# The gate's third tanh written in place in PSUM: a small convolutional stage on one NeuronCore

## The reference, cut to what matters

```
x = group_norm(hidden_states, pre_g, pre_b) + pos_emb
s1 = silu(conv2d(x, sa_w1, sa_b1, 0))              # 128 -> 16 channels
s2 = silu(conv2d(s1, sa_w2, sa_b2, 1))             # 3 x 3
spatial_weights = sigmoid(conv2d(s2, sa_w3, sa_b3, 0))   # 16 -> 1 channel
spatial_enhanced = x * spatial_weights
sh = group_norm(x, norm_g, norm_b)
```

## Time and profile before

| what | value |
|---|---|
| median of 3 runs | 4656.78 us (4655.35 to 4658.56) |
| the profiled execution | 4655.39 us |
| its span, first to last instruction | 4653.6 us |
| span of the stage `gate`, about | 1625 to 1840 us |
| mean granted TensorE clock, whole span | 0.950 of full |
| `gated`, 16 instructions | 37.2 us of DVE, 1217 ns the shortest, 2479 ns the median |
| `th3`, 16 instructions | 17.5 us of ACT, 1094 ns the median |

### The profile page before, as it was taken

How to read it: one execution, slowest core, us unless ns; L and a number is a source line. 1 busy time by engine, 2 the same in 40 slices (tenths; PEclk the granted TensorE clock), 3 DMA queues, 4 the chain that set the end, 5 groups by cost and what they waited for, 6 DMA issues and landing times. The chain is left out here.

```text
span 4653.6 us, 68684 instructions
## 1 busy us (share of the span) xinstructions
PE 4149.5 (89%) x25550; PEld 1213.7 (26%) x25550; DVE 3600.5 (77%) x4166; ACT 3118.8 (67%) x5561; POOL 1545.3 (33%) x862
## 2 busy tenths in 40 slices
PE   5999999999996776699999999999999999578888
PEld 1222222222222733122222222222222222123333
DVE  7999999999993366787777777787777777178774
ACT  2888888888886354467777777777777777334443
POOL 1111111111110033144433344444433343346666
PEclk6999999999998977799999999999999999779999
DMA  2323323223211243211122122121122110112221
GB/s 63 57 49 65 65 47 70 63 45 73 60 41 43 77 168 140 46 40 43 34 49 49 45 45 48 40 45 44 32 49 49 45 36 18 46 55 72 71 69 54
DMA packets 144281, 261.96 MB, mean 56 GB/s; under 512 B 58192, under 2 KB 58192, under 8 KB 143824
## 3 DMA queue, kind: packets, MB, share of 16 engines
q1 hardware_dynamic: 143952, 257.61, 21.9%
HBM read 155.13 MB, written 85.13 MB: 52 GB/s over the span
## 5 line engine op out<-in xcount | busy, mean ns | idle before, releaser
L703 DVE TENSOR_REDUCE c_mx<-banks 128x2 f32<-128x1024 f32 x1280 | 1524.6, 1220 | 346.3 <-PE banks L496 191.5
L596 ACT ACTIVATE c_e<-banks 128x512 f32<-128x512 f32 x2560 | 1388.3, 594 | 595.7 <-PE banks L530 323.0
L703 DVE TENSOR_REDUCE a_mx<-banks 128x2 f32<-128x1024 f32 x1024 | 1208.5, 1218 | 63.3 <-PE banks L496 53.3
L596 ACT ACTIVATE a_e<-banks 128x512 f32<-128x512 f32 x2048 | 1111.0, 594 | 178.9 <-PE banks L520 156.8
L545 PE MATMUL banks<-a_e,a_vs 128*32 128x512 f32 x4096 | 546.4, 605 | 0.2 <-ACT a_e L596 0.2
L545 PE MATMUL banks<-c_e,c_vs 128*32 128x512 f32 x4096 | 546.3, 605 | 0.0
L441 POOL TENSOR_TENSOR c_esum<-c_e,c_esum 128x1024 f32<-128x1024 f32 x224 | 527.3, 2354 | 36.7 <-ACT c_e L596 11.3
L496 PE MATMUL banks<-a_stack 48*128 48x512 f16 x2048 | 390.9, 390 | 77.1 <-DMA a_stack<-k_halves 24.9
L520 PE MATMUL banks<-a_stack 50*128 50x512 f16 x2048 | 399.6, 387 | 48.6 <-ACT a_e L596 35.1
L520 PE MATMUL banks<-c_stack 50*128 50x512 f16 x2048 | 398.6, 386 | 45.6 <-ACT c_e L596 36.0
L496 PE MATMUL banks<-c_stack 48*128 48x512 f16 x2048 | 377.0, 387 | 23.3 <-DVE c_mx L703 17.0
(11 more groups left out here) (322 smaller groups left out, 4518.0 us busy)
## 6 DMA issues: line engine op xcount, KB each, us to landing
a_stack<-q_halves SPq DMA_DIRECT2D x96, 128.0 KB, 4.4
a_stack<-k_halves SPq DMA_DIRECT2D x96, 128.0 KB, 7.6
c_stack<-q_halves SPq DMA_DIRECT2D x96, 128.0 KB, 4.3
c_stack<-k_halves SPq DMA_DIRECT2D x96, 128.0 KB, 7.2
early_x<-in_x SPq DMA_DIRECT2D x16, 512.0 KB, 9.3
a_res<-in_x SPq DMA_DIRECT2D x16, 512.0 KB, 4.1
q_halves<-a_parts SPq DMA_DIRECT2D x16, 512.0 KB, 2.9
k_halves<-a_parts SPq DMA_DIRECT2D x16, 512.0 KB, 3.8
```

Of the source, the lines that this page charges most:

```text
L596: nc.scalar.activation(e[q % 4][:, 2 * i + h, :], bank_of(n - 1 + h), ACT.Exp).then_inc(st_free, 1)
L703: nc.vector.tensor_reduce(mx[j % 2][:, :, i, qc, half], slot[:, :, :], AX.X, ALU.max).then_inc(mr_free, 1)
```

## The change

The tanh is written over its own input in the bank pair `p_s3`, and `gated` reads it there. The two SBUF tiles `th3` are gone. `th3` no longer waits for an earlier `gated`, and `conv3` of the next image, which writes `p_s3` anew, waits for the `gated` of the image before it instead of for its `th3`.

```
-        th3, gated, normed = ring("th3", 2, [P, N]), ring("gated", 2, [P, N]), ring("normed", 2, [P, N])
+        gated, normed = ring("gated", 2, [P, N]), ring("normed", 2, [P, N])
...
                 if step == "conv3":
                     pe.wait_ge(s2_ready, b + 1)
                     if b:
-                        pe.wait_ge(th3_ready, b)
+                        pe.wait_ge(gated_ready, b)
...
                 if step == "th3":
                     act.wait_ge(s3_made, b + 1)
-                    if b > 1:
-                        act.wait_ge(gated_ready, b - 1)
-                    nc.scalar.activation(th3[b % 2][:, :], flat(p_s3), ACT.Tanh, bias=halves[2], scale=0.5).then_inc(th3_ready, 1)
+                    nc.scalar.activation(flat(p_s3), flat(p_s3), ACT.Tanh, bias=halves[2], scale=0.5).then_inc(th3_ready, 1)
...
-                    nc.vector.scalar_tensor_tensor(out=gated[b % 2][:, :], in0=th3[b % 2][:, :], scalar=1.0, in1=xs[b % 3][:, :],
+                    nc.vector.scalar_tensor_tensor(out=gated[b % 2][:, :], in0=flat(p_s3), scalar=1.0, in1=xs[b % 3][:, :],
                                                    op0=ALU.add, op1=ALU.mult).then_inc(gated_ready, 1)
```

## The result

| what | before | after |
|---|---|---|
| median of 9 runs each, taken together | 4655.92 us (4653.09 to 4664.30) | 4643.47 us (4638.76 to 4646.53) |
| ratio of the times, with 95% interval | | 0.9968 (0.9959 to 0.9977) |
| span of the profiled execution | 4653.6 us | 4637.0 us |

The forecast was 4644.2 us, with a range of 4641 to 4655. The medians lie 12.4 us apart, and the ratio says 14.9 us (10.7 to 19.1). So the kernel is faster by more than the 0.2% that was set as the bound.

A forecast was written before the change was run, and what follows sets the result against it. The gate was taken as bound by a once-per-image chain of waits, with `gated` waiting for POOL; 13 x 0.98 = 12.7 less 0.1 gives 12.6 us off 4655.39, 4642.8, plus 1.4 for a median: 4644.2 us, range 4641 to 4655.

The forecast's parts named there:

- rival (4): `gated` on DVE still waits for POOL despite the PSUM input; no gain, 4656.8 us; chance 0.05.
- 13 x 0.98 = 12.7 us: Gate stage: 13 periods each lose the 0.98 us that `gated` costs the chain between `add` and `stat2`.
- 2.38 + 8.64: Gate period after the change: 2.38 us from `add` to `stat2`, 8.64 from there to the next `add`, 11.02 together.
- rival (5): More gain: `group` products and `conv3` at PE's high clock every period, 4642.9 us; chance within the likeliest case's 0.70.
- 1.31 us: Time taken for `gated` with one input in PSUM, from `a_y`; its SBUF form alone costs 1.22 us.
- estimate of 65 ns more: Skill-table cost of each `gated` reading PSUM, 62 / 0.96 = 65 ns, swallowed by the periods' cover.
- Rival (1): `th3` in place on ACT takes twice as long, 2.18 us, delaying `gated`; 4656.9 us; chance 0.07.
- 0.52 us of gap ahead of `group1`: PE's gap between `conv1` and `group1` shrinks from 1.50 us to 0.52 but stays, so the gain stands.
- rivals (2) and (3): PE's low clock bounds the gate: all periods, 4676 us, chance 0.05; or some periods, 4648 to 4654, chance 0.13.
- rival (3): Two to four low-clock PE periods, or several with `conv1` alone slow, leave 3 to 9 us gain; chance 0.13.
- 1.74 - 0.52 = 1.2 us: Loss in each gate period where `conv1` alone runs slow on PE, after the remaining gap ahead of `group1`.
- The fourteenth slow `gated`: Beside the gate's last `add`; gives nothing, because the end hangs on the last `conv1`, which waits for that `add` alone.

The follow-up runs named there:

- e2: Kernel before with PE's wait moved and `gated` reading raw `p_s3` in PSUM, the tanh still written to SBUF: 4639.84 us, ratio 0.9963 to before.
- e3: Changed kernel with the tanh still in place in PSUM but `gated` reading the position tile in SBUF: 4655.78 us, ratio 0.9999 to before.
- e6: Kernel before with `gated` due at 4.30 in place of 4.04, behind `s2` when POOL is idle: 4660.89 us, ratio 1.0009 to before.
- e5: Kernel before with the first half of `conv1` computed twice, six more matmuls an image: 4656.30 us, ratio 1.0006 to before.
- e9: Changed kernel with the in-place tanh done twice in a row: 4654.26 us, ratio 0.9994 to before.
- e1: Kernel before with only the change's two wait edits, tanh and product still in SBUF: 4657.88 us, ratio 0.9998 to before.
- e11: Changed kernel with the first half of `conv1` computed twice: 4652.28 us, ratio 0.9992 to before.

## Why the prediction was right

*The mechanism.* `gated` stood beside every `add`, with two SBUF inputs, and DVE began it only when POOL was through. The prediction read this from the pair of rows and from 2.48 against 1.22 us. The experiments show each side by itself, and rival (4) fell: PSUM read alone, 1.22 (e2); two SBUF inputs with the change's other half, 2.51 (e3); two SBUF inputs with POOL idle, 1.22 (e6). The row that the forecast had to lean on was of 128 elements; the changed kernel has the long one. By the Trainium skill, "SBUF — State Buffer", section "Who interferes with whom", a VectorE instruction with at most one SBUF input doesn't contend with GpSimd outside the two-port modes: the 13 rows of 1.225 us beside an `add` agree.

*The size.* 13 x 0.98 = 12.7 us were forecast, and the thirteen periods gave 13.8. The term is 2.38 + 8.64. The first part measured 2.39. The second came to 8.54, about the shorter of the two values that alternated before (12.09 - 3.36 = 8.73 and 11.88 - 3.36 = 8.52). The longer ones had the second group product at TensorE's low clock (0.56 us for 0.35, at a granted clock of 0.50); after the change all thirteen took 0.35. The second group products of a long and of a short period before, and of one after:

```profile
1669.92 0.56 PE L1187 MATMUL banks<-g_pair,mats_sb 128*128 128x2 f32 x2 [0.76 <-DVE g_minus L1308]
...
1681.99 0.35 PE L1187 MATMUL banks<-g_pair,mats_sb 128*128 128x2 f32 x2 [0.76 <-DVE g_minus L1308]
```

```profile
1712.75 0.35 PE L1187 MATMUL banks<-g_pair,mats_sb 128*128 128x2 f32 x2 [0.76 <-DVE g_minus L1306]
```

That is rival (5) in so far as the group products go, which the prediction put inside its own range; `conv3` and the last `conv1` still met the low clock, up to 2.08 and 3.63 us. Over the thirteen periods the granted clock rose from 0.78 to 0.87. Why the low stretches no longer meet the group products isn't settled: e5 gave TensorE less idle time (0.81 granted) and kept them. That the median came within 0.7 us of the forecast is in part luck. The forecast stood on a median of three executions, 0.9 us above that of nine, and the medians' difference (12.4 us) happens to lie nearer to the forecast's 12.6 than the gate's own 13.8.

*`gated` from PSUM.* I took 1.31 us, from `a_y`. It measured 1.225, 8 ns above its SBUF form (1.217). The estimate of 65 ns more from the table in the Trainium skill, "VectorE: DVE Perf Modes", section on the TRN2 errata, does not hold here; the measured 8 ns decide.

*`th3` in place.* 1.07 us in place of 1.09. Rival (1) fell, and e9 shows that its price was about right: 4654.26 us against 4656.9 worked out. There the product still took 1.22 us and not my 1.31, which is 0.09 x 13 = 1.2 us of the difference.

*The waits, and what is late next.* e1 shows the waits at nothing. TensorE was named as next, with 0.52 us of gap ahead of `group1` in one kind of period; it is 1.09 us in ten of thirteen, because `conv1` no longer waits in PE's queue in any of them but starts with the end of its `add`. Part of rivals (2) and (3) came true: `conv1` ran mostly at the low clock in three of the thirteen periods (3.38 to 3.43 us, granted 0.55 to 0.56), and none of them got longer. So rival (3)'s loss did not come. The slow `conv1` at 1741.39 stood behind 2.01 us of idle time, and so did the next one (2.00 us ahead of 1752.32), which ran at the high clock in 1.91 us; the idle time ahead doesn't decide the level by itself. TensorE's timeline of the slow one:

```profile
1741.39 3.40 PE L1199 MATMUL banks<-g_xs,mats_sb 128*32 128x496 f32 x12 [2.01 <-POOL g_xs L1168]
1744.73 0.38 PE L1187 MATMUL banks<-g_pair,mats_sb 128*128 128x2 f32 x2
1745.55 0.35 PE L1187 MATMUL banks<-g_pair,mats_sb 128*128 128x2 f32 x2 [0.44 <-DVE g_minus L1306]
```

`group1` is 0.34 us late (3.34 against 3.00 behind the start of `conv1`), yet the second product starts 4.16 us behind it, as in the next period (4.14). What DVE does between `pair1` and `minus1` hides the lateness. The prediction priced a slow `conv1` alone at 1.74 - 0.52 = 1.2 us. Most of that was too dear before any cover: `conv1` lost 1.49 us and the gap was 1.09, which leaves 0.40, and 0.34 were measured. The cover took these last 0.34. In e11 `group1` is 1.1 to 1.4 us late in the slow periods and the period grows by 0.7 to 1.0, so this cover holds about 0.4 us (0.2 in the two where `group1` itself took 0.59 us).

*The end.* The fourteenth slow `gated` was said to give nothing, and the gate ended 13.8 us sooner, which is what the thirteen periods gave.

## What to carry to other kernels

When a VectorE instruction with two SBUF inputs shows two durations, look at what GpSimd does at its start. If the longer ones end about one own length after GpSimd's end (here 1.1 us of 1.22), the cost is a wait, and putting one input in PSUM removed it here. Its price is not the lost duration but how much later the next link of the chain starts: 1.26 us of DVE time bought 0.98 us here, because the next instruction waits for the same `add`. Then follow the chain once around: a single due time (`shift1` ahead of `field`) was worth about as much as the whole change.

## What was not expected

- A tanh written in place in PSUM is no slower than one written to SBUF: 1.066 against 1.094 us for 128 x 1024. In e9 the second of the two in a row took 1.088.
- With 0.9 us more of matmuls in every period (e5), TensorE's low clock still met the group products. In the changed kernel it met none of them, but three of the thirteen `conv1` (3.4 us for 1.9) instead.
